# The third comparison of a search step moves from VectorE to GpSimd

## The reference

```
scores = softmax(xf @ gate_w.T, axis=-1)
vals, idx = top_k(scores.T, k)        # k = 2048 of 16384 tokens, for each of 8 experts
y = xf[idx]  ->  layer norm, fc1, gelu, fc2, times the score
xf = xf.at[idx].add(out)              # then a last layer norm
```

## Time and profile before

| | |
|---|---|
| median of three runs | 4323.76 us |
| the profiled execution | 4334.82 us, span 4333.1 us |
| GpSimd, VectorE, ScalarE, TensorE busy | 3575.5, 3741.0, 3476.0, 3545.1 us |
| stage 2 in the profile | from 3338 to 3415 us |
| seven steps on upper halves | from 3342.14 to 3365.95 us |
| eight steps on whole scores | from 3365.95 to 3397.0 us |

### The profile page before, as it was taken

The page is one execution under the profiler, slowest core; times in us unless marked ns, Lnnn a source line. Parts: engine busy times, 40 slices in busy tenths (PEclk is TensorE's granted clock), DMA queues, the critical chain, the costliest instruction groups (busy, mean ns, idle before and its releaser), DMA issues. The chain is left out here.

```text
span 4333.1 us, 57736 instructions
## 1 busy us (share of the span) xinstructions
PE 3545.1 (82%) x19574; PEld 2477.0 (57%) x19574; DVE 3741.0 (86%) x4796; ACT 3476.0 (80%) x5917; POOL 3575.5 (83%) x1883
## 2 busy tenths in 40 slices
PE   7778888888888788888888888888866399999983
PEld 3455555555555555555555555555555388888872
DVE  5899999999999999999999999999997766656655
ACT  5889999899999999999988999999883155655653
POOL 3899999999999999999999999999895266665667
PEclk9999999999999999999999999999986599999996
DMA  2667776776766677776767767666664133333346
GB/s 85 151 160 170 173 169 166 166 178 158 166 166 158 163 168 177 169 173 166 171 161 167 176 158 165 165 161 161 155 165 95 55 61 74 65 64 61 65 127 248
DMA packets 178855, 628.41 MB, mean 145 GB/s; under 512 B 33648, under 2 KB 97264, under 8 KB 119168
## 3 DMA queue, kind: packets, MB, share of 16 engines
q0 software_dynamic: 73920, 368.61, 42.3%
q1 hardware_dynamic: 104640, 256.10, 17.6%
HBM read 223.57 MB, written 68.68 MB: 67 GB/s over the span
## 5 line engine op out<-in xcount | busy, mean ns | idle before, releaser
L463 POOL TENSOR_TENSOR dbu<-du,bb 128x2048 f32<-128x2048 f32 x511 | 2429.0, 4807 | 105.3 <-DVE h L939 80.4
L939 DVE TENSOR_TENSOR_SCAN h<-da,hlast,dbu 128x512 f32<-128x512 f32 x1536 | 1867.7, 1265 | 79.1 <-POOL dbu L463 52.7
L791 PE MATMUL ht<-ident,h 128*128 128x128 f32 x8192 | 1179.6, 289 | 455.5 <-DVE h L939 167.6
L524 ACT ACTIVATE da<-dl,negA 128x512 f32<-128x512 f32 x2048 | 1413.7, 702 | 120.1 <-DVE h L939 114.6
L791 PEld LDWEIGHTS ht<-ident,h 128*128 128x128 f32 x8192 | 966.9, 147 | 868.7 <-DVE h L939 321.0
L543 ACT ACTIVATE pair<-ht,ct 128x512 f32<-128x512 f32 x896 | 592.1, 688 | 130.3 <-PE ht L791 75.0
L939 DVE TENSOR_TENSOR_SCAN h<-da,dbu 128x512 f32<-128x512 f32 x512 | 592.4, 1206 | 42.2 <-POOL dbu L463 20.1
L715 PE MATMUL spare<-xin,win 128*128 128x512 f32 x1024 | 493.5, 612 | 11.8 <-DMA xin<-in_xt 7.3
L724 PE MATMUL spare<-xh,conv 128*128 128x512 f32 x1024 | 464.0, 595 | 0.8 <-ACT xh L555 0.8
L1704 ACT ACTIVATE hraw<-f,b 128x512 f32<-128x512 f32 x256 | 176.2, 688 | 253.3 <-PE f L1787 227.8
L447 POOL DMA_DIRECT2D acc<-pair x222 | 225.1, 1014 | 143.6 <-ACT pair L543 58.3
(11 more groups left out here) (244 smaller groups left out, 5677.8 us busy)
## 6 DMA issues: line engine op xcount, KB each, us to landing
acc<-pair POOLq DMA_DIRECT2D x222, 1024.0 KB, 7.2
bb<-b_rows SPq DMA_DIRECT2D x128, 1024.0 KB, 6.4
acc<-acc POOLq DMA_DIRECT2D x64, 1024.0 KB, 7.8
dl<-du POOLq DMA_DIRECT2D x62, 512.0 KB, 5.8
x_scores<-scores_and_rows SPq DMA_DIRECT2D x33, 512.0 KB, 4.6
xin<-in_xt SPq DMA_DIRECT2D x32, 512.0 KB, 4.9
sums<-scores_and_rows SPq DMA_DIRECT2D x32, 512.0 KB, 6.3
scores_and_rows<-in_x SPq DMA_DIRECT2D x31, 512.0 KB, 3.9
```

The source lines that it names most:

```text
L463: pool.tensor_tensor(dbu[n % 2][:], du[q][:], bb[part % 2][:, m:m + 1, :].to_broadcast([P, DT, CH]), ALU.mult).then_inc(dbu_done, 1)
L524: act.activation(da[DA_SLOT[m]][:], dl[q][:, dt, :], ACT.Exp, scale=negA[:, dt, n:n + 1]).then_inc(exp_done, 1)
L791: last = te.transpose(ht[HT_SLOT[m]][:, dt * P:(dt + 1) * P], h[n % 2][:, dt, b * P:(b + 1) * P], ident[:])
L939: dve.tensor_tensor_scan(h[n % 2][:, dt, :], da[DA_SLOT[n * DT + dt]][:], dbu[n % 2][:, dt, :], start, ALU.mult, ALU.add).then_inc(scan_do ...
```

## The change

In steps 7 to 14, those on whole scores, VectorE makes the comparisons t = 0 and t = 1 and GpSimd makes t = 2. It is the same operation on the same tiles. GpSimd waits before each for the semaphore `step` at 3i, which is when the candidates are written; TensorE waits before its third group for the new semaphore `compared_pool`. The first seven steps are as they were.

```diff
+    LOW = UPPER // 2
...
+        compared_pool = a.sem("compared_by_pool")
+
+        def by_dve(i):
+
+            return TRY if i < LOW else TRY - 1
+
...
+                for i in range(LOW, STEPS):
+                    pool.wait_ge(step, 3 * i)
+                    pool.tensor_scalar(over[TRY - 1][:], sc[:], cand[:, TRY - 1:TRY].bitcast(F32), None, ALU.is_ge
+                                       ).then_inc(compared_pool, 1)
                 pool.wait_ge(chain, 6)
                 pool.tensor_tensor(chosen[:], gt[:], eq[:], ALU.add).then_inc(chosen_ok, 1)
...
-                        te.wait_ge(compared, i * TRY + t + 1)
+                        if t < by_dve(i):
+                            te.wait_ge(compared, min(i, LOW) * TRY + max(i - LOW, 0) * (TRY - 1) + t + 1)
+                        else:
+                            te.wait_ge(compared_pool, i - LOW + 1)
...
-                    for t in range(TRY):
+                    for t in range(by_dve(i)):
                         dve.tensor_scalar(over[t][:], scores[:], cand[:, t:t + 1].bitcast(F32), None, ALU.is_ge
                                           ).then_inc(compared, 1)
```

## The result

| | before | with the change |
|---|---|---|
| median, 17 runs each | 4326.25 us | 4334.68 us |
| lowest, highest | 4321.89, 4331.57 | 4326.65, 4337.85 |
| one whole-score step in the profile | 3.91 us | 4.97 us |

The account below looks back on a forecast made before the run. No engine is full; each whole-score step is a chain whose every link waits for the one before. Eight steps, 1.00 us longer each, give 4323.76 + 8.0 = 4331.8 us, range 4325.5 to 4338.5.

Parts of the forecast that it names:

- Where the time is and that nothing else moves: Only the eight whole-score steps, 31 us of 4333.1, change; the seven steps before and stage 3 stay as they were.
- The cap on a gain: If nothing blocks, the copy starts at 2.27 instead of 2.55, 0.28 us a step, 2.2 us in all; chance 0.06.
- Price of GpSimd's comparison: GpSimd's comparison of 1024 elements in a whole-score step: 0.22 us fixed and 1.30 ns an element, about 1.55 us.
- upper bound of 2.09 ns: Highest price per element for GpSimd's comparison, from four L1610 starting 0.535 us apart; 2.1 us for 1024 elements.
- the comparison is dear: Rival: GpSimd's comparison costs from 1.38 ns an element; 4335.1 us with 1.7 ns, 4338.3 with 2.09; chance 0.30.
- the cheap rival: GpSimd's comparison costs a cast's 0.82 ns an element, with blocking: 0.51 us a step, 4327.9 us; chance 0.20.
- In each pair one engine stands still until the other's instruction is done: VectorE and GpSimd block each other for whole instructions, so a step's three comparisons lie end to end.
- The order: In each whole-score step: comparison 0 on VectorE, then GpSimd's ending at 2.13 us, then comparison 1 ending at 2.69.
- its fixed 0.2 us: Part of GpSimd's comparison independent of elements, spent first while VectorE's comparison 0 runs, over before that ends at 0.75.
- The signs in the profile: Expected profile: steps of some 4.9 us, GpSimd's comparison about 2, VectorE's second drawn out, TensorE's second and third groups touching.
- The sum: With blocking, the copy of a whole-score step starts at 3.55 instead of 2.55: 1.00 us a step, 8.0 in all.

## Why the prediction was right, and where it was not

- **Where the time is and that nothing else moves:** right. The search's chain took 8.5 us more, and the eight steps, 1.06 us each, are the whole of it; the seven steps before took 23.81 us and then 23.75.
- **The cap on a gain, 0.28 us a step:** right in kind. It was worked out for a third comparison that is counted last. ScalarE went past it, 0.67 us, because its comparison was counted between VectorE's two.
- **"Price of GpSimd's comparison", 1.30 ns an element, 1.55 us:** wrong. It is 2.84 us alone, 2.5 ns an element, beyond even the upper bound of 2.09 ns. The step that failed is the choice of row: L1610 and L1204 agreed with each other and neither is a single comparison; L1610 is the quick pair. The rival "the comparison is dear" had the direction of the price and not its size, and the argument for the cheap rival, one operation where L1610 does two, points the wrong way: here one operation is the dearer. The Trainium skill's figure, page "GPSIMD Engine Reference", section "Performance pitfalls for Q7 kernels", from which the prediction made an estimate of 1.69 ns, is also below what the runs measured.
- **"In each pair one engine stands still until the other's instruction is done":** wrong for this instruction. The rows it was read from fit it, and so does the quick product and sum, but GpSimd's comparison kept VectorE off for only 0.86 of its 2.84 us, and was itself only 0.37 us longer beside VectorE's 1.41. The Trainium skill, page "SBUF — State Buffer", section "Who interferes with whom", has the pair taken for the whole instruction, and here the runs disagree with that.
- **The order:** wrong. GpSimd's started 0.05 us before VectorE's, nearly as the prediction had worked out, and went first; I had set this aside for its fixed 0.2 us. Where it started 0.02 us after VectorE's it went second.
- **The signs in the profile:** the step of some 4.9 us came (4.97). GpSimd's comparison of about 2 us (3.20), a drawn-out second comparison of VectorE's (the first was), and TensorE's second and third group touching (0.51 us apart) did not.
- **The sum, 1.00 us a step:** measured 1.06, but by two errors that cancel, which is luck. With the true price in the forecast's own model (comparison 0, then 0.05 + 1024 x 2.5 = 2.61, then 0.56 and 0.86) the copy would have started at 4.78, 2.23 us a step later or 17.8 in all, outside the range. The direction was right for half a reason: the comparison is dearer on GpSimd, and the two engines contend. What in fact made it is GpSimd's end at 3.15 us after VectorE's start, 1.07 later than the 2.08 of VectorE's third comparison before. Its price alone would give 0.71 of that (2.84 - 0.05 = 2.79), and sharing the ports gives the other 0.36.

## What to carry to other kernels

Before work goes to GpSimd, price exactly that instruction, with its number of operations; a neighbour of the same name can be two or three times cheaper. A GpSimd instruction beside VectorE's fast form holds VectorE for about its number of elements times 0.84 ns, even if nobody waits for it, and one of the slow kind can do so twice: here the step grew by 0.78 us, or by 1.62 where GpSimd went first. And where a chain of a few microseconds is to be split over engines, take one beside which VectorE runs unhindered, as ScalarE here, and let its result be consumed in the middle and not at the end.

## What was not expected of the hardware

- On GpSimd a `tensor_scalar` of 1024 float32 elements takes 2.77 to 2.85 us with one operation and 1.04 to 1.19 us with product and sum. Two operations with a comparison take 3.70 to 3.72 us.
- VectorE's fast form is held for the elements that GpSimd has (0.77 to 0.86, 0.42, 0.21 us for 1024, 512, 256), the same for 2-byte and 4-byte elements, and in the slow kind a second time near GpSimd's end, if VectorE still has a comparison to make (0.76, 0.33, 0.12 us).
- For instructions of one operation the order of the two engines turned between a start 0.05 us before VectorE's and one 0.02 us after it; product and sum went second from either.
